# Linear attention with a routed feed-forward block on one core: score products over the 64 rows that hold their quarter of the heads, two quarters in turn to two banks

## The chip, the cores and the metric

The kernel runs on one core of one Trainium2 chip. The metric is device time in microseconds (us), from one launch of the whole program. Three runs of the kernel before gave 339.87, 343.55 and 344.41 us: the median is 343.55 us.

The core has a matrix engine (TensorE, PE in the profile, with its weight loads shown apart as PEld), a vector engine (DVE), a scalar engine (ACT), a general engine (POOL) and a queue engine (SP). They run their own instruction streams and wait for each other with semaphores. TensorE reads its stationary operand and its moving operand from the on-chip memory (SBUF, 128 rows) and writes to eight PSUM banks (128 rows by 512 fp32 each).

## What is computed

One transformer block with modulation: layer norm, causal linear attention with 16 heads of width 8, a residual with a gate, layer norm, a feed-forward network with 8 experts of which each token takes one, a residual with a gate. All is fp32; x is 2 x 2048 x 128.

```python
def step(carry, qkv_t):                 # over the 2048 tokens
    S, z = carry
    qt, kt, vt = qkv_t                  # q, k = elu(.) + 1
    S = S + kt[..., :, None] * vt[..., None, :]
    z = z + kt
    num = jnp.einsum('bhi,bhij->bhj', qt, S)
    den = jnp.sum(qt * z, axis=-1, keepdims=True)
    return ((S, z), num / (den + EPS))
...
h = _layernorm(x, axis=-1) * (1 + ca) + sa
x = x + ga * _L0_attn_ref(h, L0_attn_w_attn, L0_attn_w_proj)
h = _layernorm(x, axis=-1) * (1 + cb) + sb
x = x + gb * _L0_ffn_ref(h, L0_ffn_W1, L0_ffn_W2, L0_ffn_Wg, L0_ffn_bg)
```

## The kernel before

The 4096 tokens are 32 tiles of 128. Eight groups `g` of four tiles (tiles `2b + s`, batch `b`, half `s`) go through the attention, and their rows are scattered to memory sorted by expert. After the last group, 39 tiles of the sorted rows go through the experts. The change lies in the attention alone.

Channels stand on the 128 rows: head `h` has rows 8h to 8h+7, so quarter `q` of the heads has rows 32q to 32q+31. Attention works in chunks of 64 tokens: what comes from earlier chunks goes through a running state (`core_across`, L1013 and L1020), what comes from within a chunk through score products that are masked and multiplied with v (`core_within`, L1033).

`core_scores` (L1001) makes the score products. For one tile it takes the four quarters `q` in turn. For a quarter it issues four matmuls (two chunks `n`, two `half`s). Each has a stationary operand of 128 rows by 64 columns (`k_q[:, q]`, k of that quarter, zero on all other rows) and a moving operand of 128 rows by 128 columns (two of the four masked copies `q_m` of q). The product contracts over the 128 rows; `half` picks which 64 columns of the array, and so which 64 rows of the bank, receive it. Quarter `q` goes to bank `score_bank[q % 2]`, S0 or S1. DVE then multiplies the bank with the causal mask into `probs` (`core_probs`, L654), one instruction of 128x256 for each quarter.

A call of `core_scores` in the loop takes two quarters, FIRST = (0, 1) or LAST = (2, 3), which is 8 matmuls; the trace has each fp32 matmul as two passes, so 16 passes. There are 4 tiles x 2 calls in each of 8 groups, 64 such calls. The waits: quarter number i of the whole program waits until DVE has finished the quarter i-2, which had the same bank (the wait for `probs_ready`), and DVE waits for the semaphore `score_mm` that the last matmul of each quarter raises.

`step(g)` on PE writes out the order by hand. In the order of time it has (f = g+1 is the group whose front work is done meanwhile): scores of tile (s=0,b=1) LAST; `front_x` (L950, transposes of the normalised x for f); within; `front_qkv` (L956, L958, L962); across; scores (1,0) FIRST and LAST back to back; within; `front_kt` (L971); across; scores (1,1) FIRST; `route_turn` (L1056, transposes for group g-1); scores (1,1) LAST; `route_logits` (L1062); within; across; scores (0,0) FIRST of group f; `front_den` (L979); `route_rank` (L1069, L1070); within; scores (0,0) LAST of f; across; scores (0,1) FIRST of f; `front_inv` (L987); `core_proj` (L1047). Step 0 and the last step are written out and leave parts away; steps 1 to 6 are a loop.

DVE's stream has its own order by hand. Behind the masks of a tile stand the running state (L660), y (L672), the layer-norm statistics of the rows of group g-1, q and k of group f (L631, L636), the scan and the argmax of the router (L719 to L743), the denominators and the slots (L751 to L777), and `core_x1` (L685), which reads the projection from bank F0. `front_x` of the next step writes F0 and so waits for it. ACT makes from the same banks h_t (L432), the exponentials (L439 to L445), v_n, v_m and k_q (L456 to L470), k_n (L477, which waits for L971), xhat (L424), h_t of the router (L488, which waits for L1056) and q_m (L451), in this order.

## Time and profile before

| | |
|---|---|
| median of 3 runs | 343.55 us (339.87 to 344.41) |
| span of the profiled execution | 339.4 us |
| PE busy | 285.0 us, 84% of the span |
| DVE busy | 241.9 us, 71% |
| ACT busy | 152.0 us, 45% |
| score products (L1001), PE busy | 71.9 us, 1024 passes |
| masks (L654), DVE busy | 51.6 us, 128 instructions |
| share of the chain that ended last: PE, DVE, ACT | 63%, 15%, 4% |
| of it the score products | 18% |

The profile is one execution. Start and duration of each instruction are read from it; the end of a matmul is modelled. The timeline view merges instructions of one line that follow each other, so that "x16" is 16 of them and the duration is from the first start to the last end. In square brackets it gives how long the engine sat idle before and what released it. An idle stretch of a busy engine need not cost anything, and a busy PE need not be at its peak.

The attention takes from about 30 us to 240 us; each of the steps 1 to 6 takes 24.7 us. The experts take from about 250 us to the end.

### The profile page before, as it was taken

To read this page: it belongs to the slowest core of one execution; us is meant where nothing else is said; L and a number is where in the kernel's file an instruction comes from. 1 tells how busy PE (TensorE), PEld (TensorE's weight loads), DVE (VectorE), ACT (ScalarE), POOL (GpSimd) and SP (SyncE) were. 2 spreads that over 40 slices of the span, in tenths; PEclk is the share of its full clock that TensorE was granted. 3 is DMA by queue.
4 is the path that set the end of the run, shared out by engine and by line. 5 is a ranking of instruction groups with operands and counts; after the bars stand their busy time and mean duration, and the time that the engine had idled before them with its cause. 6 is when DMAs were issued, how large, how long until landed. Compare 5 with 4: busy or idle time off the path is not lost.

```text
span 339.4 us, 10754 instructions
## 1 busy us (share of the span) xinstructions
PE 285.0 (84%) x3847; PEld 245.5 (72%) x3847; DVE 241.9 (71%) x842; ACT 152.0 (45%) x301; POOL 124.8 (37%) x142
## 2 busy tenths in 40 slices
PE   1777989999999999999999998942129999999980
PEld 1446678688688788787787887742119999999980
DVE  4974557778778778778687787663735888988880
ACT  3378491780871871861952830000023444444430
POOL 8979000303503404305305205232311546545662
PEclk9997999999999999999999999785558999999995
DMA  7990000001000001001001001000252334333410
GB/s 212 319 302 5 3 2 2 2 3 35 34 4 37 27 0 48 16 0 63 1 0 64 0 0 66 2 34 33 82 162 70 108 90 117 93 95 97 113 38 0
DMA packets 16906, 20.19 MB, mean 59 GB/s; under 512 B 2747, under 2 KB 13117, under 8 KB 16882
## 3 DMA queue, kind: packets, MB, share of 16 engines
q1 hardware_dynamic: 13040, 12.50, 13.1%
q0 software_dynamic: 2832, 6.57, 5.6%
q10 hardware_dynamic: 1010, 0.81, 0.8%
q8 instruction: 15, 0.25, 0.3%
q14 instruction: 9, 0.07, 0.1%
HBM read 12.22 MB, written 8.10 MB: 60 GB/s over the span
## 4 chain that ended last, share of the span: by engine, by line
PE 63%; DVE 15%; issue 6%; ACT 4%; POOL 3%; DMA 3%; DVEq 2%; SPq 1%; POOLq 0%; ACTq 0%
PE bank L1001 18%; PE bank L1013 5%; PE bank L1138 5%; PE bank L1147 4%; PE bank L1033 4%; PE bank L1020 4%; PE bank L956 3%; DVE k_q L885 3%; PE bank L1062 3%; PE bank L979 2%; PE bank L971 2%; ACT h_t L432 2%; POOL sorted_rows L374 2%; PE bank L962 2%; PE bank L1047 2%
## 5 line engine op out<-in xcount | busy, mean ns | idle before, releaser
L374 POOL DMA_INDIRECT sorted_rows<-row_buf,slot_i x32 | 31.6, 987 | 119.7 <-DVE slot_i L777 112.4
L1001 PE MATMUL bank<-q_m,k_q 128*64 128x128 f32 x1024 | 71.9, 284 | 2.6 <-DVE probs L654 2.0
L654 DVE TENSOR_TENSOR probs<-bank,causal 128x256 f32<-128x256 f32 x128 | 51.6, 421 | 22.8 <-PE bank L1001 21.9
L1001 PEld LDWEIGHTS bank<-q_m,k_q 128*64 128x64 f32 x1024 | 56.2, 140 | 10.5 <-DVE probs L654 5.9
L396 POOL DMA_INDIRECT out_dram<-q_m,slot_token x39 | 40.8, 1047 | 44.9 <-DVE q_m L901 27.1
L1138 PE MATMUL bank<-q_m,k_q 128*128 128x128 f32 x312 | 43.0, 283 | 0.0
L1147 PE MATMUL bank<-k_q,v_m 128*128 128x128 f32 x312 | 41.5, 276 | 0.0
L1138 PEld LDWEIGHTS bank<-q_m,k_q 128*128 128x128 f32 x312 | 39.6, 199 | 0.0
L1147 PEld LDWEIGHTS bank<-k_q,v_m 128*128 128x128 f32 x312 | 38.1, 193 | 0.4 <-DVE q_m L898 0.4
L541 ACT ACTIVATE v_m<-bank 128x512 f32<-128x512 f32 x39 | 23.3, 598 | 27.2 <-PE bank L1138 27.2
L484 ACT ACTIVATE rden<-bank 128x512 f32<-128x512 f32 x8 | 4.8, 597 | 49.7 <-PE bank L987 49.6
L880 DVE COPY k_q<-w_all 128x512 f32 x39 | 16.9, 434 | 14.0 <-PE bank L1138 8.5
L1033 PE MATMUL bank<-probs,v_m 128*32 128x64 f32 x1024 | 21.4, 225 | 2.0 <-DVE probs L654 1.6
L1131 PE MATMUL bank<-ident,v_m 128*128 128x128 f32 x39 | 11.2, 286 | 12.3 <-DMA v_m<-sorted_rows 12.3
L1013 PE MATMUL bank<-q_t,state 128*128 128x64 f32 x128 | 21.3, 289 | 0.0
L1033 PEld LDWEIGHTS bank<-probs,v_m 128*32 128x32 f32 x1024 | 16.4, 111 | 5.9 <-issue 5.5
L451 ACT ACTIVATE q_m<-q_t,quad_head 128x512 f32<-128x512 f32 x32 | 20.4, 709 | 0.0
L470 ACT ACTIVATE k_q<-k_t 32x512 f32<-32x512 f32 x32 | 20.1, 628 | 0.5
L354 POOL TENSOR_TENSOR guess<-var,minus_half 128x4 f32<-128x4 f32 x8 | 8.3, 1042 | 31.4 <-DVE var L572 31.4
L1020 PE MATMUL bank<-v_n,k_n 128*128 128x64 f32 x128 | 19.5, 275 | 0.0
L536 ACT ACTIVATE q_m<-bank 128x128 f32<-128x128 f32 x39 | 10.8, 277 | 19.3 <-PE bank L1131 19.3
L1013 PEld LDWEIGHTS bank<-q_t,state 128*128 128x128 f32 x128 | 16.9, 192 | 3.3 <-issue 1.5
(177 smaller groups left out, 510.6 us busy)
## 6 DMA issues: line engine op xcount, KB each, us to landing
v_m<-sorted_rows SPq DMA_DIRECT2D x39, 132.0 KB, 2.1
x_all<-in_L_attn_x_dram SPq DMA_DIRECT2D x16, 128.0 KB, 4.2
w_all<-in_L_ffn_W_dram SPq DMA_DIRECT2D x1, 2048.0 KB, 9.6
out_dram<-q_m,slot_token POOLq DMA_INDIRECT x39, 2.3
sorted_rows<-zeros ACTq DMA_DIRECT2D x4, 132.0 KB, 2.3
sorted_rows<-zeros SPq DMA_DIRECT2D x4, 132.0 KB, 2.5
sorted_rows<-row_buf,slot_i POOLq DMA_INDIRECT x32, 2.4
wmod_sb<-in_L_wmod_dram SPq DMA_DIRECT2D x1, 384.0 KB, 4.8
```

Of the source, the lines that this page charges most:

```text
L374: pool.indirect_dma_start(sorted_rows, bass.IndirectOffsetOnAxis(ap=slot_i[par][:, t:t + 1], axis=0), row_buf[par][:, t, :], None).then_in ...
L396: pool.indirect_dma_start(out_rows, bass.IndirectOffsetOnAxis(ap=slot_token[ring][:], axis=0), y_row[ring], None, bounds_check=B * T - 1, ...
L451: last = nc.scalar.activation(q_m[par][:, a, :], q_t[par][:], ACT.Copy, scale=quad_head[:, a:a + 1])
L470: last = nc.scalar.activation(k_q[par][rows, q, :], k_t[par][rows, :], ACT.Copy)
L541: nc.scalar.activation(gelu[par], [S0, S1][par][:].rearrange("p (k c) -> p k c", k=HC), ACT.Gelu_apprx_tanh).then_inc(gelu_ready, 1)
L654: V.tensor_tensor(probs[:, s, b, q, :], score_bank[q % 2][:, 0:QUADS * L], causal[:].rearrange("p a t -> p (a t)"), ALU.mult).then_inc(pro ...
L1001: last = mm(score_bank[q % 2][L * half:L * half + L, 2 * L * n:2 * L * n + 2 * L], k_q[par][:, q, tok:tok + L], q_m[par][:, 2 * half:2 * h ...
L1013: mm(y_bank[half][:, b * L:b * L + L], state[:, half, b, :], q_t[par][:, tok:tok + L], start=(b == 0), stop=False, skip_group_check=True)
L1020: last = mm(ST[:, b * L:(b + 1) * L], k_n[par][:, n, :], v_n[par][:, n, :], start=False, stop=True, skip_group_check=True)
L1033: last = mm(y_bank[half][32 * q:32 * q + 32, b * L:b * L + L], v_m[par][:, 2 * (2 * b + s) + half, a, 32 * q:32 * q + 32], probs[:, s, b, ...
L1138: last = mm([S0, S1][par][:, j * P:(j + 1) * P], w1_cur[wbuf][:, j * P:(j + 1) * P], h_col[par], start=True, stop=True)
L1147: last = mm([Y0, Y1][par][:, 0:C], gelu[par][:, j, :], w2_cur[wbuf][:, j, :], start=(j == 0), stop=(j == HC - 1))
```

## The change

The two quarters of a call are now 0 and 2, then 1 and 3: one from the rows 0 to 63, one from the rows 64 to 127. Each product contracts only over its 64 rows, since k_q is zero on the others. The two quarters go to two banks (q // 2) and are issued in turn, matmul by matmul. A call waits once, before its first matmul, until DVE has finished both quarters before it; the second quarter had the later wait, and it stands now for both. The very first matmul of each call, the one that carries the wait, contracts over only the 32 rows of its quarter. The masks take the quarters in the new order, and the first tile of the program makes its four quarters in two calls.

```diff
-FIRST, LAST = (0, 1), (2, 3)
+FIRST, LAST = (0, 2), (1, 3)
+ORDER = FIRST + LAST
...
-            def core_probs(g, s, b, quads=range(QUADS)):
+            def core_probs(g, s, b, quads=ORDER):
                 wait_ge(dve, y_mm, 4 * g + 2 * s - 1)
                 for q in quads:
-                    dve.wait_ge(score_mm, 16 * g + 8 * s + 4 * b + q + 1)
-                    V.tensor_tensor(probs[:, s, b, q, :], score_bank[q % 2][:, 0:QUADS * L],
+                    dve.wait_ge(score_mm, 16 * g + 8 * s + 4 * b + ORDER.index(q) + 1)
+                    V.tensor_tensor(probs[:, s, b, q, :], score_bank[q // 2][:, 0:QUADS * L],
                                     causal[:].rearrange("p a t -> p (a t)"), ALU.mult).then_inc(probs_ready, 1)
...
-            def core_scores(g, par, s, b, quads=range(QUADS)):
+            def core_scores(g, par, s, b, quads):
...
-                for q in quads:
-
-                    pe.wait_ge(probs_ready, 16 * g + 8 * s + 4 * b + q + 1)
-                    for n in range(2):
-                        tok = t * P + n * L
-                        for half in range(2):
-                            last = mm(score_bank[q % 2][L * half:L * half + L, 2 * L * n:2 * L * n + 2 * L],
-                                      k_q[par][:, q, tok:tok + L], q_m[par][:, 2 * half:2 * half + 2, tok:tok + L],
-                                      start=True, stop=True)
-                    last.then_inc(score_mm, 1)
+                pe.wait_ge(probs_ready, 16 * g + 8 * s + 4 * b + ORDER.index(quads[1]) + 1)
+                for n in range(2):
+                    tok = t * P + n * L
+                    for half in range(2):
+                        for q in quads:
+                            rows = slice(L * (q // 2), L * (q // 2) + L)
+                            if n == half == 0 and q == quads[0]:
+                                rows = slice(32 * q, 32 * q + 32)
+                            last = mm(score_bank[q // 2][L * half:L * half + L, 2 * L * n:2 * L * n + 2 * L],
+                                      k_q[par][rows, q, tok:tok + L],
+                                      q_m[par][rows, 2 * half:2 * half + 2, tok:tok + L], start=True, stop=True)
+                            if n == 1 and half == 1:
+                                last.then_inc(score_mm, 1)
...
-            core_scores(0, 0, 0, 0)
+            core_scores(0, 0, 0, 0, FIRST)
+            core_scores(0, 0, 0, 0, LAST)
```

On PE, in step 0 (the loop's steps have the same with a register instruction for the value of each wait), this is the place of the scores (1,0) FIRST and LAST, between `core_across` (the last row of L1020) and `core_within`. The first two names are the bank that is written and what it is made of; 64x128 is the size of a product. Before:

```order
L1020 MATMUL bank<-v_n,k_n 128x64 x2
L1001 MATMUL bank<-q_m,k_q 64x128 [waits probs_ready]
L1001 MATMUL bank<-q_m,k_q 64x128 x3
L1001 MATMUL bank<-q_m,k_q 64x128 [waits probs_ready]
L1001 MATMUL bank<-q_m,k_q 64x128 x3
L1001 MATMUL bank<-q_m,k_q 64x128 [waits probs_ready]
L1001 MATMUL bank<-q_m,k_q 64x128 x3
L1001 MATMUL bank<-q_m,k_q 64x128 [waits probs_ready]
L1001 MATMUL bank<-q_m,k_q 64x128 x3
L1033 MATMUL bank<-probs,v_m 32x64 [waits probs_ready,masks]
```

The same place of the changed program:

```order
L1024 MATMUL bank<-v_n,k_n 128x64 x2
L1004 MATMUL bank<-q_m,k_q 64x128 [waits probs_ready]
L1004 MATMUL bank<-q_m,k_q 64x128 x7
L1004 MATMUL bank<-q_m,k_q 64x128 [waits probs_ready]
L1004 MATMUL bank<-q_m,k_q 64x128 x7
L1037 MATMUL bank<-probs,v_m 32x64 [waits probs_ready,masks]
```

Sixteen matmuls stand there in both, with four waits before and two now; each of the two now waits for both banks, so no matmul of LAST can start while DVE still reads the second bank of FIRST.

The second place on PE is the scores (0,0) LAST and (0,1) FIRST of the next group with `core_across` between them, and `front_inv` behind. Before:

```order
L1001 MATMUL bank<-q_m,k_q 64x128 [waits probs_ready,kq_ready,qm_ready]
L1001 MATMUL bank<-q_m,k_q 64x128 x3
L1001 MATMUL bank<-q_m,k_q 64x128 [waits probs_ready]
L1001 MATMUL bank<-q_m,k_q 64x128 x3
L1013 MATMUL bank<-q_t,state 128x64 [waits y_ready,state_ready]
L1013 MATMUL bank<-q_t,state 128x64
L1020 MATMUL bank<-v_n,k_n 128x64 [waits v_ready,kn_ready]
L1020 MATMUL bank<-v_n,k_n 128x64
L1001 MATMUL bank<-q_m,k_q 64x128 [waits probs_ready]
L1001 MATMUL bank<-q_m,k_q 64x128 x3
L1001 MATMUL bank<-q_m,k_q 64x128 [waits probs_ready]
L1001 MATMUL bank<-q_m,k_q 64x128 x3
```

In the changed program:

```order
L1004 MATMUL bank<-q_m,k_q 64x128 [waits probs_ready,kq_ready,qm_ready]
L1004 MATMUL bank<-q_m,k_q 64x128 x7
L1017 MATMUL bank<-q_t,state 128x64 [waits y_ready,state_ready]
L1017 MATMUL bank<-q_t,state 128x64
L1024 MATMUL bank<-v_n,k_n 128x64 [waits v_ready,kn_ready]
L1024 MATMUL bank<-v_n,k_n 128x64
L1004 MATMUL bank<-q_m,k_q 64x128 [waits probs_ready]
L1004 MATMUL bank<-q_m,k_q 64x128 x7
```

Nothing changes its place; the wait in the middle of each call is gone, and the wait at its head now asks for one more mask of DVE. DVE's stream keeps its 128 masks at their places, in the order of quarters 0, 2, 1, 3.

## Rows read from the trace of the kernel before

**Rows 1.** The page: its head, and the group of the score products.

```profile
span 339.4 us, 10754 instructions
...
L1001 PE MATMUL bank<-q_m,k_q 128*64 128x128 f32 x1024 | 71.9, 284 | 2.6 <-DVE probs L654 2.0
```

**Rows 2.** Busy by stretch, one period from L950 to L950 (length; PE, PEld, DVE, ACT, POOL; clock).

```profile
133.92:158.62 24.70, 24.14 (x398) 19.97 (x397) 18.93 (x65) 14.02 (x27) 7.07 (x8) 1.00 0.06 22
```

**Rows 3.** Timeline, PE, two stretches: start, duration, engine, line, count.

```profile
149.87 0.55 PE L1001 MATMUL bank<-q_m,k_q 128*64 128x128 f32 x6
...
149.87 1.09 PE L1001 MATMUL bank<-q_m,k_q 128*64 128x128 f32 x16
```

**Rows 4.** Timeline, PE, where the form of the products changes, full clock.

```profile
149.33 0.61 PE L1020 MATMUL bank<-v_n,k_n 128*128 128x64 f32 x4
```

**Rows 5.** Timeline, PE, near the program's start, lower clock.

```profile
7.48 1.02 PE L931 MATMUL bank<-c_silu,wmod_sb 128*128 128x2 f32 x4 [7.48 <-DVE c_bc L602]
8.43 0.59 PE L932 MATMUL bank<-bg_row,ones 1*128 1x8 f32 x2
8.95 3.78 PE L934 MATMUL bank<-wmod_sb,c_bc 128*128 128x512 f32 x4
12.53 0.63 PE L937 MATMUL bank<-zeros 128*128 128x128 f32 x2
12.95 0.63 PE L938 MATMUL bank<-zeros 128*128 128x128 f32 x2
```

**Rows 6.** Timeline, scores (1,0) FIRST and LAST with their masks, and what follows.

```profile
139.72 2.28 PE L1001 MATMUL bank<-q_m,k_q 128*64 128x128 f32 x32
...
140.42 0.86 DVE L654 TENSOR_TENSOR probs<-bank,causal 128x256 f32<-128x256 f32 x2
140.90 0.85 PEld L1001 LDWEIGHTS bank<-q_m,k_q 128*64 128x64 f32 x16 [0.33 <-DVE probs L654]
...
141.61 0.86 DVE L654 TENSOR_TENSOR probs<-bank,causal 128x256 f32<-128x256 f32 x2 [0.32 <-PE bank L1001]
141.93 0.49 PEld L1033 LDWEIGHTS bank<-probs,v_m 128*32 128x32 f32 x32 [0.17 <-issue]
...
143.71 1.20 ACT L477 ACTIVATE k_n<-bank 64x512 f32<-64x512 f32 x2 [0.20 <-PE bank L971]
```

**Rows 7.** Timeline, scores (1,1) FIRST and LAST, masks, logits.

```profile
144.63 1.09 PE L1001 MATMUL bank<-q_m,k_q 128*64 128x128 f32 x16
...
145.33 0.86 DVE L654 TENSOR_TENSOR probs<-bank,causal 128x256 f32<-128x256 f32 x2 [1.07 <-PE bank L1001]
...
146.24 0.85 PEld L1001 LDWEIGHTS bank<-q_m,k_q 128*64 128x64 f32 x16 [0.17 <-DVE probs L654]
...
147.26 0.97 PEld L1062 LDWEIGHTS bank<-wg_sb,h_t 128*128 128x128 f32 x8 [0.17 <-ACT h_t L488]
...
148.36 0.19 DVE L727 TENSOR_TENSOR logit<-bank,bg_bc 128x32 f32<-128x32 f32 x1 [0.22 <-PE bank L1062]
```

**Rows 8.** Timeline one step earlier, from the denominators to the next `front_x`.

```profile
126.28 0.97 PEld L979 LDWEIGHTS bank<-block,qz 128*128 128x128 f32 x8 [0.25 <-DVE qz L738]
...
129.91 0.76 DVE L654 TENSOR_TENSOR probs<-bank,causal 128x256 f32<-128x256 f32 x2
130.38 0.85 PEld L1001 LDWEIGHTS bank<-q_m,k_q 128*64 128x64 f32 x16
...
133.11 0.69 DVE L685 TENSOR_TENSOR row_buf<-x_all,bank 128x512 f32<-128x512 f32 x1 [1.08 <-PE bank L1047]
...
133.92 0.42 PEld L950 LDWEIGHTS bank<-ident,xhat 128*128 128x128 f32 x4 [0.18 <-issue]
```

**Rows 9.** Timeline, last step: masks of (1,0), its LAST at the lower clock.

```profile
212.46 0.74 DVE L654 TENSOR_TENSOR probs<-bank,causal 128x256 f32<-128x256 f32 x2
212.93 1.57 PEld L1001 LDWEIGHTS bank<-q_m,k_q 128*64 128x64 f32 x16 [1.76 <-DVE probs L654]
212.93 1.98 PE L1001 MATMUL bank<-q_m,k_q 128*64 128x128 f32 x16 [1.52 <-DVE probs L654]
```

## The prediction

> **What bounds the kernel now.** I read the page first: 339.4 us, of which the score products hold PE for 71.9 us [rows 1]. The busy time by stretch then shows that a period of the attention takes 24.70 us, with PE busy for 24.14 us of it at the full clock, DVE for 18.93 and ACT for 14.02 [rows 2]. That looks like a kernel bound by PE. The timeline says otherwise in places, and the places are what counts, since the change makes PE's calls shorter and their waits stricter.
>
> How long is a call? Two passes run at once, one in each 64-column strip: six passes take 0.55 us and sixteen take 1.09 us, so ten more passes, five rounds of two, take 0.54, or 0.11 us a round [rows 3]. A run of k rounds in this form takes 0.55 + 0.11 (k - 3) us; that is 0.44 for two rounds, 0.65 for four, 1.09 for eight.
>
> What happens where the form changes? Before the score call the products have 128 columns; they end at 149.33 + 0.61 = 149.94, and the call starts at 149.87, 0.07 us before that end [rows 4, 3]. The same 0.07 stands at a change of the rows alone: the products of L931 (128 rows) end at 8.50 and L932 (1 row, same 128 columns) starts at 8.43; L932 ends at 9.02 and L934 starts at 8.95. Where the form stays, L937 ends at 13.16 and L938 starts at 12.95, 0.21 us before the end, with the work overlapping [rows 5]. So a new form waits for the old one to run out, and a change of rows is a change of form.
>
> Where does DVE hold PE? A mask starts 0.70 us after its call (139.72 to 140.42), and the second call of (1,0) starts at 140.90, as soon as the first of the two masks is done (140.42 + 0.42 + 0.06); PE leaves the pair at 141.93 [rows 6]. In (1,1), FIRST starts at 144.63, its masks at 145.33, LAST at 146.24, the logits' products at 147.26 [rows 7]. The denominators' products wait for DVE (126.28), and (0,1) FIRST starts at 130.38 while the two masks of (0,0) LAST run from 129.91 to 130.67 [rows 8]. ACT makes k_n at 143.71 right when L971 is through [rows 6]. So DVE and ACT are chained to PE at nearly every call.
>
> **What a call becomes.** Its first matmul contracts over 32 rows, the seven others over 64: one more change of form, inside the call. The first matmul is two passes alone, 0.44 us as the run of two rounds, and 0.07 before its end, at 0.37, the second form begins. Fourteen passes remain: four in three of the array's four corners (two strips of rows by two of columns), two in the fourth. If the corners work at once as the column strips do, that is four rounds, 0.65 us. The call then ends at 0.37 + 0.65 = 1.02 us instead of 1.09: halving the products' time (0.44 us off) is nearly eaten by the two lonely passes and the drain. No row shows two row strips at once. The bounds are four rounds (0.65) and eight (1.09, if row strips take turns, as the last column strip has eight passes); I take four, since it is the same array, and carry eight as a rival. Whether 32 to 64 rows drains has bounds as well: no drain gives a call of four rounds, 0.65 us; the rows of L932 give 1.02. I take the drain, because L932 is a change of rows alone.
>
> The masks come later. Before, the first bank was through after four rounds (0.65) and its mask began at 0.70, 0.05 later. Now both banks get their last pass in the last round, at 1.02: the masks begin at 1.07 (+0.37). Both are then ready, and two masks back to back take 0.76 [rows 8], to 1.83; 0.06 later, at 1.89, the next call may start, if nothing else stands between. PE itself is free 0.07 earlier than before.
>
> By the Trainium skill (TensorE: Matmul & The Clock Gate, Measured speedup vs the span model) four row tiles gave 3.07 and not 4 times the speed; a round would by that be some 0.14 us, the call 0.1 us longer, and the total about 5 us above mine. No run here shows it, and it is an estimate from that page.
>
> **One period, walked through.** All shifts are against the same event before.
> 1. (1,0): LAST may start 1.89 instead of 1.18 us after FIRST. PE leaves the pair at 1.89 + 0.95 = 2.84 instead of 2.21 (141.93 - 139.72): +0.6. L1033, L971 and ACT's k_n follow at +0.6, since ACT already waited for L971 [rows 6].
> 2. (1,1): FIRST +0.6. Its masks end 1.83 after it; LAST starts 1.89 instead of 1.61 after FIRST: +0.9. The logits' products leave 0.07 earlier than that, +0.8. On DVE the masks of LAST ended at 146.24 + 0.70 + 0.86 = 147.80, and the logits started 0.56 later, of which 0.22 were idle; now the masks end at 147.14 + 1.83 = 148.97, and the logits start 0.34 later at 149.3, +0.9 [rows 7].
> 3. From there DVE is dense and leads. The products of L979, which waited for it at 126.28, are +0.9, and PE's faster (0,0) FIRST buys nothing.
> 4. (0,0) LAST +0.9. (0,1) FIRST started at 130.38, but now needs the second mask as well, which ends at 129.91 + 0.76 = 130.67, so 130.73 + 0.9: +1.25. PE's own arrival, +0.85, is earlier, so the stricter wait decides [rows 8].
> 5. FIRST is 0.07 shorter: `front_inv`, the projection and `core_x1` are +1.2. (0,1) LAST also is 0.07 shorter, which brings `front_x` to +1.1; `core_x1` ends at 133.11 + 0.69 = 133.80 against its start at 133.92, so it wouldn't let more than 0.1 through [rows 8].
>
> So a period is 1.1 us longer: 0.6 from the pair back to back, 0.3 from (1,1), 0.35 from the stricter wait in (0,1), less the 0.07 at some calls.
>
> **The sum.** Periods led by steps 1 to 6: 6 x 1.1 = 6.7 us (unrounded 1.12). The start (four quarters of the first tile back to back, then (0,1) FIRST and LAST with nothing but a wait between them) is two pairs of the kind of point 1, 1.1 us together as DVE waits cover some. Step 0 has two such pairs, (1,0) and (1,1), and a milder end: 1.1 us. The last step: (1,0) LAST starts at 212.93, after the first mask (212.46 + 0.42 + 0.05); now after the second, 213.20 + 0.05, +0.3, and its (1,1) costs 0.3 more, with masks and logits behind, together 0.8 [rows 9, 7]. Sum 1.1 + 1.1 + 6.7 + 0.8 = 9.7 us. After the last step the chain goes through slots and scatters on DVE and POOL, and then the experts; the change touches none of it, so the shift is carried whole. On the span that is 339.4 + 9.7 = 349.1. The median of the runs is 343.55, 4.1 us above the span; on it, 343.55 + 9.7 = 353.3, and I say 353.
>
> What costs nothing: the masks' other order and banks; the waits that are gone (register instructions of PE, beside passes). Nothing is added to DVE or ACT.
>
> **The rivals.**
> *No drain between 32 and 64 rows.* For it: they are not the pair of forms that the rows show. A call is 0.65, the masks begin at 0.70 and end at 1.46, the next call at 1.52 instead of 1.18 and PE leaves at 1.52 + 0.58 = 2.10 instead of 2.21: -0.1. ACT and DVE then lead to L979 (-0.1); (0,1) FIRST waits for the second mask, +0.25; it is 0.44 shorter, so the projection and `core_x1` are at -0.2, and `front_x` waits for `core_x1`. A period is 0.2 us shorter, eight of them 1.8: 341.7 us, not slower. It decides from a drain of less than about 0.1 us. That is also the answer to the plain count of 64 calls x 0.44 = 28 us less (316 us): it holds only where PE alone leads. The Trainium skill (TensorEngine Tiling, Theoretical Speedup) has "Up to 2x" for a contraction of 64 rows or less; by that page the time would be that 316, an estimate, and the rows of the masks speak against it.
> *Row strips take turns.* The second form takes 1.09 and not 0.65: a call 1.46, masks 0.44 later. Twice in point 1, twice in point 2, one in point 5 and the next step's start: about six times 0.44 = 2.6 us a period more, eight of them 21: 374 us. Against it: column strips do work at once.
> *The clock falls.* PE idles about 1 us more in each back-to-back pair. In the last step, after an idle of 1.52 us, a call of 16 passes took 1.98 and not 1.09 us [rows 9]. If a fall like that comes once in each period, with some 1.5 us lost in each (0.9 in a call, the rest in its neighbours), that is 7 x 1.5 = 10: 363 us. Against it: the period has the full clock now with 0.5 us idle [rows 2].
>
> **How the numbers follow.** Mine 0.64; no drain, or a drain so short that the gain pays for the waits, 0.17; turns, fully or in part, 0.11; clock 0.06; faster by over 2% 0.02, where DVE's masks would have to move up as well. My own range is 350 to 357 (period 0.7 to 1.5 us longer). Leaving out the full turns and the lower part of no drain, the 8-in-10 range is 344 to 362. 2% is 6.9 us and about what can be told from no change here: mine lies above it but for its lowest tenth. So slower 0.64 x 0.9 + 0.11 + 0.06 = 0.75; same 0.06 + 0.17 = 0.23; faster 0.02.
>
> **What would show it.** Right: a call (now L1004) has a first run of 2 passes and then 14 within 1.02 us, and the masks start 1.07 after the call; PE waits about 0.8 us for probs between (1,0) FIRST and LAST; the period is 25.8 us. Wrong: a call of 0.65 (no drain) or 1.46 (turns), a mask 0.7 after its call, a period of 24.7 or less, or an ACT or DVE wait that had slack which I took for none. The experts must take the same time as before.

## The result, and the profile after

The changed kernel takes 384.62 us (383.96 to 385.85) beside 343.41 for the kernel before: 1.126 times as long, 95% interval 1.117 to 1.135. Every ratio in this document is formed from the faster executions of both kernels alone, so it can differ a little from the quotient of the medians beside it. The prediction was 353, in a range of 344 to 362. The direction was right. The size was not: 9.7 us were forecast and 41.2 measured.

The page of the changed kernel, head, TensorE's and DVE's share, PE's busy tenths and its clock in 40 slices, and the two groups that answer to [rows 1]:

```profile
span 382.2 us, 10707 instructions
...
PE 317.6 (83%) x3847; PEld 259.2 (68%) x3847; DVE 238.7 (62%) x842; ACT 151.9 (40%) x301; POOL 124.3 (33%) x142
...
PE   2758979989989989999999999879240999999990
...
PEclk9965795897798797698798699765555899999997
...
L1004 PE MATMUL bank<-q_m,k_q 64*64 64x128 f32 (+1 forms) x1024 | 81.7, 339 | 12.3 <-DVE probs L655 12.3
L655 DVE TENSOR_TENSOR probs<-bank,causal 128x256 f32<-128x256 f32 x128 | 48.2, 418 | 58.2 <-PE bank L1004 57.8
```

The calls were meant to be a little shorter, and their busy time rose from 71.9 to 81.7 us. PE's wait for `probs` rose from 2.6 to 12.3 us; in the back-to-back pair shown below it is 0.85, where about 0.8 were forecast. The clock row is what was not: the same row of the kernel before reads

```profile
PEclk9997999999999999999999999785558999999995
```

Before, slices 5 to 27, which hold nearly all of the attention, show the full clock but for one dip in the last step (slices 26 and 27); after, every step has slices of 6 to 8 tenths. The busy time by stretch, one row for each period from `front_x` (now L951) to the next, answers to [rows 2]; columns as there, the third number from the end is the granted clock:

```profile
39.20:71.32 32.12, 29.17 (x383) 22.12 (x381) 13.87 (x34) 13.41 (x26) 0.00 (x0) 0.73 0.01 2
71.32:101.12 29.80, 28.16 (x399) 21.55 (x397) 18.60 (x65) 14.01 (x27) 7.16 (x7) 0.83 0.06 20
101.12:129.53 28.41, 26.77 (x399) 20.58 (x397) 18.63 (x64) 14.00 (x27) 7.06 (x7) 0.88 0.06 21
129.53:159.28 29.75, 28.09 (x396) 21.48 (x396) 18.55 (x64) 14.00 (x27) 7.07 (x7) 0.83 0.05 18
```

A period is 28.4 or 29.8 us, where 25.8 were forecast and 24.70 stood before. The clock has two levels, 1.2 and 2.4 GHz, 0.50 and 1.00 in this column. A mean of 0.83 over 29.75 us therefore means that (1 - 0.83) / 0.5 of it, 10.1 us, ran at the lower one; 0.88 over 28.41 is 6.8 us.

A call at the full clock, one fall, and the calls behind it, in the timeline of the changed kernel:

```profile
135.33 1.02 PE L1004 MATMUL bank<-q_m,k_q 32*64 32x128 f32 x16
...
135.69 0.42 PEld L1004 LDWEIGHTS bank<-q_m,k_q 64*64 64x64 f32 x14 [0.17 <-issue]
136.39 0.75 DVE L655 TENSOR_TENSOR probs<-bank,causal 128x256 f32<-128x256 f32 x2 [0.39 <-PE bank L1004]
...
137.20 1.02 PE L1004 MATMUL bank<-q_m,k_q 32*64 32x128 f32 x16 [0.85 <-DVE probs L655]
...
138.14 0.49 PEld L1037 LDWEIGHTS bank<-probs,v_m 128*32 128x32 f32 x32 [0.17 <-issue]
...
144.68 0.65 PE L1037 MATMUL bank<-probs,v_m 128*32 128x64 f32 x32
...
148.91 1.08 PE L1037 MATMUL bank<-probs,v_m 128*32 128x64 f32 x32
...
149.93 1.74 PE L1004 MATMUL bank<-q_m,k_q 32*64 32x128 f32 x16
```

The second form starts 0.36 us after the first (forecast 0.37), a call takes 1.02 (forecast 1.02), its masks start after 1.06 (forecast 1.07), the second call of the pair after 1.87 (forecast 1.89), and PE leaves the pair after 2.81 (forecast 2.84). All that was worked out for the full clock is there. Then, from 148.7 on, the same `core_within` takes 1.08 instead of 0.65 us and a call 1.74 instead of 1.02. The busy time on both sides of that point:

```profile
129.53:148.70 19.17, 17.51 (x296) 13.29 (x296) 13.39 (x46) 13.40 (x26) 3.13 (x3) 1.00 0.00 0
148.70:158.90 10.20, 10.20 (x96) 7.97 (x98) 5.16 (x20) 0.60 (x1) 3.94 (x4) 0.50 0.15 53
```

PE was busy for 91% of the 19.17 us ahead of the fall (for 5.64 of the last 5.70 us), and for all of the 10.20 us at half the clock. It does not fall behind an idle stretch, as the third rival of the prediction had it.

Where the 42.8 us of the spans (382.2 and 339.4) stand, cut at `front_x` of the same steps:

| stretch | before | after | more | forecast |
|---|---|---|---|---|
| first `front_x` (14.86) to the third | 44.94 | 56.46 | 11.5 | 2.2 |
| five periods | 123.51 | 146.11 | 22.6 | 5.6 |
| from there to the end | 156.09 | 164.77 | 8.7 | 1.9 |

The last row holds step 6, the last step, and the experts, which the change does not touch. The experts' first product starts at 252.22 us before and at 295.26 after; the first line is of the kernel before, the second of the changed one:

```profile
252.22 0.45 PE L1131 MATMUL bank<-ident,v_m 128*128 128x128 f32 x1 [11.70 <-DMA v_m<-sorted_rows]
```

```profile
295.26 0.45 PE L1136 MATMUL bank<-ident,v_m 128*128 128x128 f32 x1 [11.65 <-DMA v_m<-sorted_rows]
```

From there to the end it is 87.2 us before (339.4 - 252.2) and 86.9 after (382.2 - 295.3), so the experts take the same time, and the 8.7 us lie in step 6 and the last step. There too the clock differs: before, it stood at 0.50 for 30.7 us, from the end of the attention's products to some 5 us into the experts'; after, for 48.0 us that begin some 19 us before the attention's last products end (269.7) and reach some 4 us into the experts'.

```profile
226.60:257.30 30.70, 8.54 (x36) 7.65 (x37) 14.16 (x61) 3.40 (x7) 7.61 (x8) 0.50 0.30 95
```

```profile
251.00:299.00 48.00, 24.82 (x214) 20.57 (x215) 22.14 (x89) 3.73 (x7) 10.44 (x11) 0.50 0.17 58
```

The first row is of the kernel before, the second of the changed one: 8.54 us of PE's work lay in the slow stretch, now 24.82. This fall, unlike those of the steps, begins behind an idle of PE: 1.92 us ahead of the call at 251.38.

### The profile page after: what moved, and what is told of

Read it like the earlier page. It is cut to its first block, busy times and chain, and to the rows that moved or that the text cites. A ratio compares the mean times of both kernels' runs of the same rounds, so it can differ in the third digit from the quotient of the medians.

```text
span 382.2 us, 10707 instructions
## 1 busy us (share of the span) xinstructions
PE 317.6 (83%) x3847; PEld 259.2 (68%) x3847; DVE 238.7 (62%) x842; ACT 151.9 (40%) x301; POOL 124.3 (33%) x142
## 4 chain that ended last, share of the span: by engine, by line
PE 61%; DVE 19%; issue 6%; DMA 4%; ACT 3%; POOL 3%; DVEq 1%; SPq 1%; POOLq 0%; ACTq 0%
PE bank L1004 19%; PE bank L1017 5%; PE bank L1143 5%; PE bank L1024 4%; PE bank L1152 4%; DVE probs L655 3%; PE bank L1037 3%; PE bank L1051 3%; PE bank L980 3%; PE bank L957 3%; DVE z_t L720 2%; PE bank L988 2%; DVE k_q L886 2%; PE bank L963 2%; PE bank L972 2%
## 5 line engine op out<-in xcount | busy, mean ns | idle before, releaser
L1004 PE MATMUL bank<-q_m,k_q 64*64 64x128 f32 (+1 forms) x1024 | 81.7, 339 | 12.3 <-DVE probs L655 12.3
L655 DVE TENSOR_TENSOR probs<-bank,causal 128x256 f32<-128x256 f32 x128 | 48.2, 418 | 58.2 <-PE bank L1004 57.8
L1004 PEld LDWEIGHTS bank<-q_m,k_q 64*64 64x64 f32 (+1 forms) x1024 | 48.2, 161 | 36.7 <-issue 19.0
L1037 PE MATMUL bank<-probs,v_m 128*32 128x64 f32 x1024 | 24.4, 245 | 4.0 <-DVE probs L655 4.0
L1017 PE MATMUL bank<-q_t,state 128*128 128x64 f32 x128 | 25.9, 336 | 0.0
L1024 PE MATMUL bank<-v_n,k_n 128*128 128x64 f32 x128 | 24.5, 325 | 0.0
L1037 PEld LDWEIGHTS bank<-probs,v_m 128*32 128x32 f32 x1024 | 18.9, 124 | 8.1 <-issue 7.6
L1017 PEld LDWEIGHTS bank<-q_t,state 128*128 128x128 f32 x128 | 21.0, 233 | 4.7 <-issue 3.0
L1024 PEld LDWEIGHTS bank<-v_n,k_n 128*128 128x128 f32 x128 | 21.8, 240 | 0.0
```

What stands on the lines that cost most here:

```text
L655: V.tensor_tensor(probs[:, s, b, q, :], score_bank[q // 2][:, 0:QUADS * L], causal[:].rearrange("p a t -> p (a t)"), ALU.mult).then_inc(pr ...
L1004: last = mm(score_bank[q // 2][L * half:L * half + L, 2 * L * n:2 * L * n + 2 * L], k_q[par][rows, q, tok:tok + L], q_m[par][rows, 2 * hal ...
L1017: mm(y_bank[half][:, b * L:b * L + L], state[:, half, b, :], q_t[par][:, tok:tok + L], start=(b == 0), stop=False, skip_group_check=True)
L1024: last = mm(ST[:, b * L:(b + 1) * L], k_n[par][:, n, :], v_n[par][:, n, :], start=False, stop=True, skip_group_check=True)
L1037: last = mm(y_bank[half][32 * q:32 * q + 32, b * L:b * L + L], v_m[par][:, 2 * (2 * b + s) + half, a, 32 * q:32 * q + 32], probs[:, s, b, ...
```

## The experiments

Twelve kernels ran. Three theories stood at the start: A, in which the costs of the drain and the waits are as worked out and the clock falls because the shorter calls keep the array **streaming for a shorter time**; and B, **waits**, in which the clock falls because PE idles in the stricter waits. The third, **rows in use**, was a rival for the third run alone: in it a product over fewer of the array's 128 rows counts for less in what decides the clock, whatever PE's busy time is. Later expectations call rows in use C1 and streaming time C2. Where a kernel is built from the kernel before, this is said.

**All products over 128 rows.** Order, banks and waits as changed.

```diff
-                            rows = slice(L * (q // 2), L * (q // 2) + L)
-                            if n == half == 0 and q == quads[0]:
-                                rows = slice(32 * q, 32 * q + 32)
+                            rows = slice(0, P)
```

> The changed kernel with every score product contracting over all 128 rows again; quarters, banks, issue in turn and the one wait for both banks stay as changed. Theory A (the row form costs a drain and two lonely passes and the stricter wait delays DVE, and the rest of the loss is the clock falling because the 64-row calls keep the array streaming for a shorter time): a call is 1.09 us, both banks are through at its end, the stricter waits cost about 1.6 us a period, the clock stays at its higher level through steps 1 to 6, and the time is about 356 us. Rival B (the clock falls because PE idles in the stricter waits): these waits are here too and longer, the clock falls in each step as in the changed kernel, and the time is 380 to 390 us.

It takes 359.58 us, 1.044 times the kernel before (1.034 to 1.053). One period of it:

```profile
118.83:145.15 26.32, 24.62 (x398) 20.38 (x396) 18.43 (x64) 14.01 (x27) 7.07 (x8) 1.00 0.06 21
```

The period is 1.6 us longer than before at the full clock, with the waits of the change and PE's idle of it: the page has PE waiting 13.1 us for `probs`, even more than the 12.3 of the changed kernel. So the waits cost what a walk gives for them (1.6 us a period were expected), and their idle does not make the clock fall in the steps: theory B is out there. A call takes 1.14 us in this order, and not the 1.09 expected. The start is another matter. From the first `front_x` (14.86) to the third (66.15) this kernel takes 51.3 us, 6.3 more than the kernel before, with a mean clock of 0.70 up to 39.95, where it is 0.92 before. So over half of the 11.5 us that the changed kernel loses there are lost with all rows in use as well.

**No first product over 32 rows.** The call's wait is put on a semaphore instruction ahead of it, and all eight products contract over 64 rows.

```diff
+                pe.sem_inc(call_head, 1)
                 for n in range(2):
...
-                            if n == half == 0 and q == quads[0]:
-                                rows = slice(32 * q, 32 * q + 32)
```

> The changed kernel without the 32-row first product: all eight products of a call contract over 64 rows; the wait stands on a semaphore instruction ahead of the call. Measures whether the four corners of the array work at once without a change of form inside the call. Theory A: a call of 16 passes takes 0.65 us, masks start 0.70 us after it; if the clock held, the time would be 342 us; since the calls stream even shorter than in the changed kernel, the clock falls as often or more, and the time is 365 to 380 us. Rival B (idle in the waits is what lowers the clock): the waits between FIRST and LAST of tile (1,0) are 0.3 us shorter, the clock falls less often, 345 to 360 us.

Its median is 360.21 us, with runs from 350.7 to 363.0, too far apart for a ratio. The timeline has the call, and the busy time one period with and one without a long stretch at the lower clock:

```profile
76.17 0.67 PE L1004 MATMUL bank<-q_m,k_q 64*64 64x128 f32 x16
```

```profile
141.50:169.82 28.32, 23.86 (x396) 19.10 (x397) 18.32 (x64) 14.02 (x27) 8.47 (x9) 0.85 0.10 32
116.63:141.50 24.87, 21.20 (x400) 16.86 (x397) 18.67 (x65) 14.02 (x27) 5.66 (x6) 0.99 0.04 15
```

A call takes 0.67 us, where 0.65 was worked out for four rounds: the four corners work at once, and the rival in which row strips take turns is out. The calls are shorter than in the changed kernel and the clock falls less often, not more: theory A had expected 365 to 380 us and missed. The time is at the edge of the 345 to 360 of theory B, which the run over 128 rows had put out. The 0.35 us between 0.67 and 1.02 are the price of the first product over 32 rows and its drain. And 24.87 us at nearly the full clock beside 24.70 [rows 2] is what 0.42 us off each call brings together with the stricter waits: nothing. PE is busy for only 21.20 of the 24.87, so its time does not set the period; that DVE's masks and ACT do is read from the waits, not tested. The plain count of 28 us less was wrong for this reason as well, clock apart.

**The first product over 128 rows, with other numbers in k_q.** The edit below, and also the copies `k_q<-k_t` on ACT over all 128 rows, so that k_q is no longer zero outside its quarter and the scores are not the reference's.

```diff
                             if n == half == 0 and q == quads[0]:
-                                rows = slice(32 * q, 32 * q + 32)
+                                rows = slice(0, P)
```

> The changed kernel with its first product of each call over 128 rows and not 32; everything else as changed. The change of form inside the call stays. Theory A (any two row forms cost the same drain): a call is 1.02 us as in the changed kernel, masks at the same place, and the time is within 2% of the changed kernel's 384.6 us. Rival (the 32-row form is special, or the number of rows in use holds up the clock): the call differs from 1.02 us, or the clock falls less and the time is under 375 us.

It takes 361.86 us, 1.061 (1.053 to 1.069). Its calls take 1.02 us as in the changed kernel, so the change of form inside the call costs the same; but the time is not within 2% of 384.6, and its last four periods run at the full clock. Rows in use is the theory that had this (under 375 us):

```profile
147.38:173.15 25.77, 23.76 (x396) 18.06 (x397) 18.37 (x64) 13.69 (x27) 7.07 (x8) 1.00 0.06 21
```

This is the changed kernel's step without its falls: 25.77 us, where the prediction had 25.8. With it the clock's price can be read: (29.75 - 25.77) / 10.1 and (28.41 - 25.77) / 6.8 both are 0.39 us for each microsecond at the lower level (an estimate, since this run's copies also took ACT 0.3 us less a period).

**The first product over 128 rows, alone.** Since the run above had two differences, they were run apart.

> The changed kernel, with the first product of each call over all 128 rows of k_q (zero outside the quarter's 32) instead of the 32. The run named e3_first128 had a second difference: the copies k_q<-k_t were made over all 128 rows, so its products also met non-zero numbers in rows that are zero in the changed kernel. This run has the first difference alone. If the rows in use decide the granted clock, it repeats that run: 358 to 366 us, full clock in the later steps with a period of 25.8 us. If the numbers in those rows decide (products of zeros count for little), it is near the changed kernel: 378 to 388 us, with 7 to 10 us of each period at the lower clock.

It takes 381.85 us on a chip on which the kernel before took 357.03 and not 340 to 343; the ratio is 1.072 (1.066 to 1.078). Three of its periods:

```profile
72.47:98.66 26.19, 23.80 (x399) 18.06 (x396) 18.48 (x65) 14.04 (x27) 6.21 (x6) 1.00 0.04 13
98.66:128.46 29.80, 25.42 (x396) 18.55 (x397) 18.79 (x64) 14.15 (x27) 7.60 (x8) 0.94 0.07 24
...
128.46:156.25 27.79, 23.69 (x396) 18.06 (x396) 18.62 (x64) 14.04 (x27) 7.06 (x8) 1.00 0.05 19
```

The clock is at its upper level but for (1 - 0.94) / 0.5 x 29.8, some 3.6 us, in one of these periods, beside 6.8 to 10.1 in each of the changed kernel. The 27.79 us at the full clock are 2.0 more than 25.77, and the waits of the steps name something that no other trace here shows (total, times, longest):

```profile
DVE probs L655 <- remote: 7.1, 5, 1.4
```

Five times DVE's first mask of a step waits 1.4 us for what the trace only calls remote. What that is stays open; it makes the absolute times of this chip unfit to compare. The median taken by itself lies in the span expected if the numbers decide (378 to 388); but on this chip the kernel before is some 15 us longer too, and the ratio, 1.072, is nearer to the 1.061 of the run before than to 1.126. The time alone does not settle it. The clock of the five periods, 0 to 3.6 us at the lower level where that theory had 7 to 10, speaks for rows in use. The two stretches ahead of them do not: from 14.90 to 72.47 us this run has 57.6 us and a clock of 0.59 and 0.74, like the changed kernel (56.5 us, 0.65 and 0.73) and unlike the run before (51.1 us, 0.68 and 0.91).

**Only the copies over 128 rows.** The other half of that run: the rows of the changed kernel, but other numbers in them.

```diff
                 for q in range(QUADS):
-                    rows = slice(32 * q, 32 * q + 32)
+                    rows = slice(0, P)
                     last = nc.scalar.activation(k_q[par][rows, q, :], k_t[par][rows, :], ACT.Copy)
```

> The changed kernel with only the second difference: the copies k_q<-k_t go over all 128 rows, so that the products over 64 rows meet non-zero numbers of the neighbouring quarter too; rows, banks, order and waits are as in the changed kernel, and the scores are not the reference's for that reason. If the rows in use decide: as the changed kernel, 380 to 388 us. If the numbers in the rows decide: 358 to 368 us, with most steps at the full clock. Both halfway (370 to 376) would say that each counts.

Its four executions took 386.5 us twice and 395 us twice, on the same chip as the one before. The median, 390.66, is above the 380 to 388 that rows in use had for it, the first two lie inside, and all are far from the 358 to 368 expected if the numbers decide. Two periods of it, from one of the shorter executions, in which no wait for something remote shows:

```profile
159.85:189.63 29.78, 28.10 (x396) 21.52 (x396) 18.56 (x64) 13.72 (x27) 7.07 (x7) 0.83 0.05 18
189.63:218.03 28.40, 26.75 (x399) 20.56 (x396) 18.61 (x64) 13.71 (x27) 7.07 (x7) 0.88 0.05 19
```

They are the changed kernel's periods to the hundredth of the clock. Non-zero numbers in the rows in use don't hold the clock, and rows full of zeros do (the kernel over 128 rows contracts mostly over zeros): in the steps of these kernels it is the rows that a product is told to use, not what stands in them.

**A pair that differs in the rows alone.** Both are the kernel before, with its own order, banks and waits, and a semaphore instruction that carries the wait of each quarter (the first line below). The control keeps 128 rows; the other has the rest of the edit too, and contracts over the 64 rows that hold its quarter.

```diff
+                    pe.sem_inc(call_head, 1)
...
+                            rows = slice(L * (q // 2), L * (q // 2) + L)
...
-                                      k_q[par][:, q, tok:tok + L], q_m[par][:, 2 * half:2 * half + 2, tok:tok + L],
+                                      k_q[par][rows, q, tok:tok + L],
+                                      q_m[par][rows, 2 * half:2 * half + 2, tok:tok + L],
```

> The kernel before with one addition: each quarter's wait stands on a semaphore instruction of its own, which raises a semaphore that nothing reads. It is the control for the next run. Each theory expects it within 1% of before (340.3 us in the last comparison), a period of 24.7 to 24.9 us, and no fall of the clock in steps 1 to 6.

> The control with each quarter's products over the 64 rows that hold it, but in the order, banks and waits of before: quarters 0 and 1 both lie in rows 0 to 63, so two strips of columns work at once as before and a call stays at eight rounds, 1.09 us. Only the number of rows in use differs from the control. Theory C1 (what holds the clock up is how much of the array is in use, rows included): the clock falls in some of steps 1 to 6, and the time is 350 to 380 us. Theory C2 (only how long the array streams counts): the same calls for the same time, no fall, 340 to 344 us.

The control takes 346.37 us, 1.014 (1.007 to 1.021), a little over the 1% that was allowed for it: three periods have the 24.9 us expected, one has 25.4, and one has 29.1, with a pause of PE of 3.52 us at 159.2 for which the profile names nothing. Over 64 rows it is 389.14 us (385.04 to 394.57), 42.8 more than the control in the medians, and 38.7 more even from its fastest execution to the control's slowest. That is above the 350 to 380 of C1, and C2, with 340 to 344, is out. A call of the control, and a call over 64 rows, both at the full clock:

```profile
96.32 1.09 PE L1003 MATMUL bank<-q_m,k_q 128*64 128x128 f32 x16
```

```profile
106.29 1.09 PE L1004 MATMUL bank<-q_m,k_q 64*64 64x128 f32 x16
```

The call is the same 1.09 us: two quarters that use the same rows one after the other gain nothing, and lose nothing, by leaving out the other 64. The stretch from 30 to 240 us of the control and then of the other:

```profile
30.00:240.00 210.00, 188.94 (x3071) 156.97 (x3071) 149.02 (x499) 99.22 (x191) 54.40 (x56) 0.97 0.06 20
```

```profile
30.00:240.00 210.00, 205.42 (x2763) 170.10 (x2761) 130.91 (x417) 98.03 (x189) 42.41 (x44) 0.79 0.04 14
```

PE is busy for 90% of it in the control and for 98% over 64 rows, and yet the clock is 0.97 in the first and 0.79 in the second (the kernel before has 0.96 in the same stretch). Part of these 98% is the slower clock itself, and the control is through with the attention before 240 us; period by period the two are as busy as each other, 97% in the control and 98% over 64 rows:

```profile
85.51:110.43 24.92, 24.21 (x398) 20.06 (x397) 19.04 (x65) 14.01 (x27) 7.24 (x8) 1.00 0.08 27
```

```profile
126.91:156.63 29.72, 29.07 (x399) 24.20 (x397) 19.50 (x65) 14.01 (x27) 7.07 (x7) 0.82 0.06 20
```

Order, banks, waits, calls and numbers are the same. This is the pair that settles that the rows of the products alone can bring the falls. The Trainium skill (TensorE: Matmul & The Clock Gate, What's actually happening) says that the clock is set by how busy the engine has been recently; that would give the second of this pair at least the clock of the first, if busy time were what is meant, and the measurement decides against that reading.

Rows are not all of it. The kernel without the 32-row product also has all its score products over 64 rows, and in the same stretch its clock is higher, with PE less busy:

```profile
30.00:240.00 210.00, 181.61 (x3020) 145.03 (x3024) 137.65 (x468) 98.44 (x188) 49.35 (x51) 0.86 0.05 17
```

It takes 360.2 us and this one 389.1. What differs is the order, the banks and the waits: there, two products over different rows run at once and a call takes 0.67 us; here, the rows take turns and it takes 1.09.

**32 rows everywhere.** In the changed kernel, and in the kernel before with its own order.

```diff
+                            rows = slice(32 * q, 32 * q + 32)
```

> The changed kernel with all products over the 32 rows of their quarter, so no change of form inside a call, and the wait stays on the first product. Calls, waits and timing should be those of the run without the 32-row first product (call 0.65 us, period near 24.9 at the full clock, 360.2 us in all); the rows in use are half of it. C1: more falls of the clock than there, 365 to 385 us. C2: the same number of falls, 356 to 363 us.

> The kernel before with its own order, banks and a wait for each quarter; only the contraction is cut to the 32 rows of the quarter. Quarters 0 and 1 then lie in different strips of rows and have different banks, so they can run at once where the waits allow. If the clock held, the period would be 24.3 us and the time 337 us. C1: 32 of 128 rows in use and shorter streaming, the clock falls in most steps, 365 to 385 us. C2: streaming is shorter as in the changed kernel without its first product, falls in about half the steps, 350 to 362 us.

They take 388.78 us, 1.145 (1.135 to 1.154), and 389.74 us, 1.144 (1.135 to 1.153), both above the 365 to 385 of C1 and far from C2. A period of each:

```profile
190.04:220.23 30.19, 28.17 (x400) 22.94 (x396) 18.95 (x64) 14.01 (x27) 7.05 (x7) 0.73 0.05 18
```

```profile
159.26:189.46 30.20, 28.78 (x400) 23.61 (x397) 19.10 (x64) 14.01 (x27) 7.06 (x7) 0.73 0.05 18
```

With 32 rows the clock is 0.73, 16.3 us of a period at the lower level, beside 6.8 to 10.1 in the changed kernel. Two orders and two sets of waits give the same here. The first of the two is a second pair in rows, beside the kernel without the 32-row product: its call at the full clock takes 0.67 us too and has no change of form inside, and 32 rows instead of 64 turn 360.2 into 388.8 us (only the instruction that carries the wait differs besides). That also speaks against the rival in which changes of form lower the clock: this pair has equally many, and the run with the first product over 128 rows kept the one inside the call and lost its falls in four periods.

**Half of the tiles over 128 rows.** The changed kernel, with the tiles s=0 (their calls stand where the falls begin) over 128 rows, and its mirror with s=1.

```diff
+                            if s == 0:
+                                rows = slice(0, P)
```

> The changed kernel with all 128 rows for the tiles with s = 0, that is the four calls of a step that stand before and after the start of each fall, and the changed form for the four calls of the tiles with s = 1. C1: half of the lost array use is back where the falls began; few or no falls in steps 1 to 6, period 25.9 to 26.1 us, time 354 to 362 us. Rival (falls depend on the waits of tile (1,0), which are unchanged here): falls in each step, 378 to 386 us.

> The mirror of the run before: all 128 rows for the tiles with s = 1, the changed form for those with s = 0. C1: the falls began behind the calls (0,0), which keep the changed form, but the calls (1,1) just before them have all rows; fewer falls than in the changed kernel, 362 to 378 us. If the place near the fall did not matter, the time would be that of the run with s = 0.

They take 373.38 us, 1.093 (1.087 to 1.099), and 372.96 us, 1.094 (1.085 to 1.102). The forecast that covering the place of the falls is enough, 354 to 362, missed. Of the 0.082 between the changed kernel's ratio (1.126) and that of all 128 rows (1.044), the calls nearest the falls take back 0.033 and the ones farther off 0.032. A period of the first, two of its mirror:

```profile
155.46:182.88 27.42, 25.62 (x398) 20.47 (x396) 18.49 (x64) 14.00 (x27) 7.07 (x8) 0.94 0.05 20
```

```profile
67.54:93.70 26.16, 24.23 (x399) 19.18 (x396) 18.50 (x65) 14.00 (x27) 5.82 (x6) 1.00 0.04 13
155.11:185.16 30.05, 28.48 (x399) 22.39 (x396) 18.59 (x64) 14.01 (x27) 7.06 (x7) 0.84 0.05 18
```

The first has a short fall in each step, some 3.3 us, which now begins in the calls of tile (1,0), behind PE's wait of 0.85 us; the mirror has steps with none and then steps of 9.6. The profiled execution of the mirror is of its longer ones (span 380.7), so its steps are read as a pattern only. Which calls of a step decide when the clock falls isn't settled by these two.

**Fillers.** The changed kernel with six idle products of 128x128x128 in each step, three of them in PE's wait between (1,0) FIRST and LAST. They write an unused part of a bank and change what stands in the rest of it, so the output isn't the reference's.

```diff
+            def fill(g, u, count):
+                pe.wait_ge(state_ready, 4 * g + u + 1)
+                for _ in range(count):
+                    mm(ST[:, 2 * P:3 * P], wqkv[:, 0:C], wqkv[:, 0:C], start=True, stop=True, skip_group_check=True)
```

> The changed kernel with idle work added on PE: six products of 128x128 by 128 columns in each step, three between the scores (1,0) FIRST and LAST, one before (1,1) LAST, two before the third core_within, written to an unused part of a bank and read by nothing. Theory C1 (the clock follows how much of the array is in use): more work on the path, about 0.5 us a period, but the clock holds in most periods; periods of 26.2 to 26.5 us, time 355 to 363 us, so the kernel gets faster than the changed one (384.6) by doing more. Rival (the clock falls for the drains and changes of form, of which there are now more): falls stay, 385 to 395 us.

It takes 385.74 us, 1.133 (1.124 to 1.141): nothing is won. C1, which had 355 to 363 for it, missed, and the number is the rival's, 385 to 395; what speaks against that rival's mechanism is the runs over 32 rows. Two periods, from an execution of 393.5 us, one of the longer ones:

```profile
136.23:163.45 27.22, 26.70 (x411) 20.34 (x408) 18.66 (x64) 14.01 (x27) 5.91 (x6) 0.94 0.04 12
163.45:194.24 30.79, 29.89 (x408) 22.90 (x408) 18.75 (x64) 14.01 (x27) 8.22 (x9) 0.83 0.09 30
```

The two kinds of period have 3.3 and 10.5 us at the lower clock, 6.9 in the mean, beside 6.8 and 10.1, or 8.5, in the changed kernel: a little less. At 0.39 us each that is 0.6 us won, and about as much goes for the fillers. Filling PE's idle isn't what was lacking; PE was not idle. A few products over all rows were not enough either; whether many more would hold the clock wasn't tried.

## Why the prediction was wrong, step by step

**Right: the call.** "The call then ends at 0.37 + 0.65 = 1.02 us": measured 0.36 to the second form, 1.02 to the end. The rivals without a drain and with strips that take turns had said 0.65 and 1.46. The kernel without the 32-row product has the 0.67 that belongs to four rounds, so both halves of the sum are shown apart. The prediction set beside its four rounds an estimate from the Trainium skill (TensorE: Matmul & The Clock Gate, Measured speedup vs the span model), a call 0.1 us longer; the 0.67 us say that the four corners cost 0.02 more than four rounds of two strips.

**Right: the masks and the waits.** Masks at 1.06 (forecast 1.07), the next call at 1.87 (1.89), the pair left at 2.81 (2.84). "So a period is 1.1 us longer": 25.77 against 24.70, in the run whose steps have the full clock. That run had the first product over other rows and other numbers in k_q, but the same calls of 1.02 us; the one over 128 rows with its calls of 1.14 gives 26.32. The direction, slower, was right for this reason, but the 9.7 us that it gives are only a quarter of the loss. What the first rival made of a call without the drain did not come out: the period was to be 0.2 us shorter than before, and with the call of 0.67 us it is 0.17 longer, at a clock of 0.99.

**Wrong: "The clock falls" with a chance of 0.06 and 1.5 us a period.** This is the step that failed, in its mechanism, chance and price. The mechanism was idle of PE in the back-to-back pair, taken from the last step of the kernel before [rows 9]. But the kernel over 128 rows has that idle and no fall in the steps, and the falls of the changed kernel begin in a stretch with 91% busy, away from the pair. The argument against the rival, "the period has the full clock now with 0.5 us idle", looked at idle alone. What the change does is in its diff: it halves, in a quarter of PE's work, the rows that a product uses. I counted what that does to the time of a call, and never asked what it does to the clock. Halving the rows alone brings falls with nothing else changed, 0.82 instead of 1.00 in a period of the pair and 389.1 instead of 346.4 us. The price was too low as well: 6.8 to 10.1 us a period at the lower level at 0.39 us each are 2.6 to 4.0 us, and not 1.5.

**Where the rest stands.** "The experts must take the same time as before": they did, 86.9 and 87.2 us, and the shift is carried whole. Of the 33.1 us between measured and forecast spans (42.8 - 9.7) the five middle periods have 17.0, the start 9.3 and step 6 with the last step 6.8. At the start a second term of the sum was mis-sized, and not by the rows alone: 2.2 us were forecast up to the third `front_x`, and the kernel over 128 rows loses 6.3 there.

**Wrong: the range.** Its upper end, 362, was made of the drain and part of the turns. With the clock rival sized as measured it would have had to reach past 380; nothing in the rows of before excluded such a fall, and it got 0.06.

**How sure.** Shown: that rows in use alone turn 346 into 389 us (the pair), that with 128 rows the changed order and its idle bring no falls in the steps, and that other numbers in the rows in use don't hold the clock (the copies alone). Argued only: that the fall in the last step has the same cause, since it begins behind an idle of PE. Open: why the same products over 64 rows hold the clock better when they run at once (0.86 and 0.79); why the clock is low at the start, where even the control has 0.69 up to its second `front_x` and the kernel before 0.92; which products of a step decide when the clock falls; and the waits for something remote on one chip. No version here beats the kernel before; the best of the changed ones near the full clock, 24.87 us a period, is no shorter than its 24.70.

## What to carry to other kernels

A matmul that contracts over fewer rows is not free even where its time stays the same: leaving the zero rows out of a quarter of PE's work cost about 40 us of 346 in the pair, through the clock and not through the call. Before slicing a contraction or packing small tiles, ask first whether PE's time sets the period at all (the masks' row and the waits tell it), and then compare the clock row of the page before and after, not only the busy times. A form of its own for the first product of a call cost 0.35 us here, beside a call of 0.67.

## What was not expected of the hardware

- Granted clock and rows in use: with the same calls of 1.09 us, 0.97 with 128 rows and 0.79 with 64, over the same 210 us. With 32 rows a period has 0.73. With 64 rows but two products over different rows at once it is 0.86, so how they run counts as well.
- It falls and stays low while PE is busy: 1.00 for 5.70 us in which PE was busy for 5.64, then 0.50 for 10.2 us in which it was busy for 10.20.
- Rows full of zeros count as rows in use (1.00 in the periods of the kernel over 128 rows); non-zero numbers in 64 rows don't replace the others (0.83 and 0.88 with either).
- Four products of 64 rows by 64 columns run at once in the four corners: 16 passes in 0.67 us, beside 1.09 in two column strips.
- A microsecond at half the clock cost the changed kernel some 0.39 us, an estimate from its periods and those of the run at the full clock, and not the 0.5 that half the clock would cost a kernel of TensorE's work alone.
